# A fused four-block transformer kernel on one core: float32 scores in four row groups, gate weights broadcast by transfers, bias at the eviction, depool by gather, scalings on GpSimd, and a new order of steps

## The reference, cut to what matters

```
x = x + tanh(g0) * xattn(ctx, LN(x))          # 8 heads of 16, keys/values from ctx (256 wide), key mask
x = x + tanh(g1) * routed_attn(LN(x))         # softmax(mean(x @ Wr + br)) -> 4 of 16 heads of 64, per batch
x = x + tanh(g2) * (rmsnorm(LN(x)) @ W_in + b_in + scan(rmsnorm(ctx)[..., :128])[plug])
x = x + tanh(g3) * moe(LN(x))                 # 8 experts, 2 per token, and a shared expert

# scan: s[t] = exp(-dt) * s[t-1] + dt * bcoef * v[t];  plug[t] = clip(count of boundaries up to t, minus 1, 0, 255)
# moe, per expert e, with w the gate weight of the token for e and m its 0/1 mask:
#   h  = silu((w x) @ w1[e].T + b1[e]);   x2 = h @ w2[e].T + b2[e]
#   x3 = (w x) @ w3[e].T + b3[e];         y += x2 * x3 * m
```

## Time and profile before

| what | value |
|---|---|
| three runs | 242.54, 243.12, 247.97 us; median 243.12 |
| the profiled execution | span 242.8 us, 3827 instructions |
| TensorE matmul / weight load busy | 211.0 us (87%) / 152.9 us |
| DVE, ACT, POOL busy | 151.1, 104.6, 54.0 us |
| DMA | 17139 packets, 12.45 MB, mean 51 GB/s |

### The profile page before, as it was taken

One profiled execution on the slowest core, in us unless ns is written; L12 is line 12 of the kernel. 1 busy time (PEld: TensorE's weight loads), 2 busy tenths in 40 slices (PEclk: granted clock), 3 DMA queues, 4 the chain that ended last, 5 costly groups with the idle time before them and its releaser, 6 DMA issues.

```text
span 242.8 us, 3827 instructions
## 1 busy us (share of the span) xinstructions
PE 211.0 (87%) x1154; PEld 152.9 (63%) x1154; DVE 151.1 (62%) x464; ACT 104.6 (43%) x283; POOL 54.0 (22%) x95
## 2 busy tenths in 40 slices
PE   0786479699878679979999979999999999999995
PEld 0564366567556455757665756767786768686764
DVE  4469855547492794776558458858984764474432
ACT  2000038155204186435374546775915732483330
POOL 1360200441041000220200351114112351323332
PEclk9995555955797999996599999999999999999999
DMA  6826288011122121000011001100000000000001
GB/s 198 293 82 195 79 230 327 1 65 54 33 44 72 65 45 25 3 1 0 1 37 33 0 0 37 34 0 3 22 0 0 4 1 22 0 3 0 0 0 43
DMA packets 17139, 12.45 MB, mean 51 GB/s; under 512 B 9024, under 2 KB 16416, under 8 KB 16992
## 3 DMA queue, kind: packets, MB, share of 16 engines
q1 hardware_dynamic: 14912, 6.90, 9.9%
q10 hardware_dynamic: 2208, 5.32, 6.7%
HBM read 8.44 MB, written 0.52 MB: 37 GB/s over the span
## 4 chain that ended last, share of the span: by engine, by line
PE 52%; DVE 1%; issue 1%; ACT 0%; ACTq 0%; DVEq 0%
PE dve_bank L655 7%; PE act_bank L647 7%; PE act_bank L648 6%; PE act_bank L650 4%; PE act_bank L594 3%; PE dve_bank L584 3%; PE act_bank L576 3%; PE dve_bank L640 2%; PE dve_bank L615 2%; PE dve_bank L669 2%; PE act_bank L660 2%; PE act_bank L449 2%; PE act_bank L561 1%; PE act_bank L512 1%; PE dve_bank L660 1%; PE dve_bank L612 1%
## 5 line engine op out<-in xcount | busy, mean ns | idle before, releaser
L769 ACT ACTIVATE hx<-act_bank,we 128x256 f32<-128x256 f32 x32 | 15.2, 475 | 36.1 <-PE act_bank L650 36.1
L1065 POOL TENSOR_TENSOR ctok<-ctok,cT 128x256 f32<-128x256 f32 x28 | 20.4, 729 | 44.6 <-DVE cT L994 43.5
L913 DVE TENSOR_REDUCE mx<-dve_bank 128x2 f32<-128x512 f32 x32 | 20.7, 686 | 10.4 <-PE dve_bank L496 10.3
L725 ACT ACTIVATE pT<-act_bank 128x512 f32<-128x512 f32 x32 | 17.6, 596 | 15.1 <-PE act_bank L512 14.9
L994 DVE SCALAR_TENSOR_TENSOR cT<-dve_bank,we,hx 128x256 f32<-128x256 f32 x32 | 15.0, 482 | 10.8 <-PE dve_bank L655 10.8
L1021 POOL TENSOR_SCALAR veps<-mv 128x2 f32<-128x2 f32 x16 | 3.1, 191 | 83.9 <-DVE mv L849 83.7
L647 PE MATMUL act_bank<-xw,we 128*128 128x256 f32 x64 | 20.3, 399 | 0.0
L655 PE MATMUL dve_bank<-hx,we 128*128 128x256 f32 x64 | 19.5, 404 | 0.2 <-ACT hx L770 0.2
L987 DVE TENSOR_TENSOR xw<-xnT,dve_bank 128x512 f32<-128x512 f32 x16 | 10.9, 684 | 13.3 <-PE dve_bank L640 13.3
L648 PE MATMUL act_bank<-xw,we 128*128 128x256 f32 x64 | 19.0, 379 | 0.0
L496 PE MATMUL dve_bank<-kstack,qstack 49*128 49x256 f32 x64 | 14.9, 368 | 4.5 <-DMA qstack<-parts 4.5
(11 more groups left out here) (165 smaller groups left out, 448.2 us busy)
## 6 DMA issues: line engine op xcount, KB each, us to landing
we<-pack_e ACTq DMA_DIRECT2D x1, 1932.0 KB, 11.2
kstack<-parts SPq DMA_DIRECT2D x24, 64.0 KB, 2.6
qstack<-parts SPq DMA_DIRECT2D x24, 64.0 KB, 2.6
w2h<-head_weights SPq DMA_DIRECT2D x16, 96.0 KB, 2.4
cT<-ctx_features SPq DMA_DIRECT2D x4, 256.0 KB, 4.2
ctok<-ctx_tokens ACTq DMA_DIRECT2D x1, 1024.0 KB, 6.8
wb<-pack_b ACTq DMA_DIRECT2D x1, 594.5 KB, 6.4
xs<-x_tokens SPq DMA_DIRECT2D x4, 128.0 KB, 3.3
```

The lines of the kernel that those rows point to most:

```text
L725: act.activation(pT1[:, i].rearrange("p c t -> p (c t)"), bank[:], ACT.Exp, scale=HD1 ** -0.5).then_inc(act_done, 1)
L769: act.activation(hx[:, k % EXPERT_BUFS, 0, :], bank[:, 0:T], ACT.Silu, bias=X("b1")[:, i:i + 1])
L913: dve.tensor_reduce(mx[:, b, :, i], bank[:].rearrange("p (t s) -> p t s", t=TT), AX.X, ALU.max).then_inc(dve_done, 1)
L1065: ins = pool.tensor_tensor(yT[:, b % 2, :], yT[:, b % 2, :], prod[:, k % EXPERT_BUFS, :], ALU.add)
```

## The change

- **Scores.** s1 and st1 are float32, without the split, a head on 16 rows plus mask and maximum row (17 and 18 rows), four heads at once on four row groups of 32; a batch is two s1 steps and two st1 steps, each with four banks. Rings are 4 and 4 banks. K and Q are spread by four DMAs each and four mask rows, the maxima by one DMA, all on SP. ks and qs are set to -1 and 1 once, in place of constant rows.
- **Gate weights.** wide is gone. After gate_t, SP issues eight DMAs a batch, each spreading one row of gT (one partition) over 128 partitions of wbc, and a step xw on DVE multiplies from SBUF. gpack has 16 rows. xw has three buffers.
- **b3.** ACT adds it at the eviction, for all tokens. What that adds for tokens outside the expert is taken out again by a table, ktab = (w2 silu(b1) + b2) * b3, made once, and one matmul of 8 rows by mask minus 1 per token tile in y4.
- **Depool.** DVE scales the scan's result by the gate and adds the bias, SP stores it in DRAM, POOL gathers its rows by plug (eight indirect DMAs of 64 KB in all), and base of block three adds them. y3 keeps only the projection; plan_c is made once for all batches.
- **GpSimd.** norm's scaling, with a shift = -mean*rstd ahead of it, scale2 and base go to POOL; base is a step of its own. One-scalar operations on POOL get a second operation (times 1.0).
- **Others.** s2 goes in pairs of heads; half of the pT2 copies go to ACT; x1 to x3 have buffers for all batches; loads are issued at the start, batches 1 to 3 and ctok on ACT's queue; waits for read buffers are stated anew; ORDER is new (its line breaks are kept).

```diff
-ACT_RING, DVE_RING = 3, 5
+ACT_RING, DVE_RING = 4, 4
...
 ORDER = """
+stat:0.0 norm:0.0 gates:0.0 kv:0.0 q:0.0 base:0.0 kv:1.0 stat:1.0 s1:0.0 s1:0.1 norm:1.0 q:1.0 max1:0.0
+plan_a:0.0 stat:2.0 s1:1.0 u:0.0 st1:0.0 s1:1.1 st1:0.1 pv1:0.0 depool:0.0 pv1:0.1 max1:1.0 heads1:0.0 o1:0.0
+plan_b:0.0 y1:0.0 norm:2.0 st1:1.0 stat:0.1 q:2.0 norm:0.1 route:0.0 kv:2.0 ktab:0.0 st1:1.1 s1:2.0 consts:0.0
+qkv2:0.0 depool:1.0 s2:0.0 plan_c:0.0 s2:0.1 scale2:0.0 s1:2.1 scale2:0.1 gather:0.0 pv1:1.0 pv1:1.1 kv:3.0
...
+o1:2.0 base:2.0 stat:1.2 y1:2.0 stat:2.1 st1:3.0 gate:0.0 norm:2.1 norm:1.2 route:2.0 y3:1.0 st1:3.1
+gate_t:0.0 stat:1.3 pv1:3.0 gather:3.0 pv1:3.1 qkv2:2.0 base:2.1 norm:1.3 s2:2.0 s2:2.1 xw:0.0 scale2:2.0
+gate:1.0 scale2:2.1 heads1:3.0 up:0.0 pt2:2.0 pt2:2.1 up:0.1 pt2:2.2 pt2:2.3 xw:0.1 down:0.0 pv2:2.0 pv2:2.1
+o1:3.0 gate_t:1.0 down:0.1 y2:2.0 up:0.2 xw:0.2 base:2.2 base:3.0 stat:2.2 y1:3.0 stat:3.1 xw:0.3 shared:0.0
...
+gate:3.0 xw:2.2 up:2.2 y4:1.0 down:2.0 down:2.1 xw:2.3 gate_t:3.0 up:2.3 up:2.4 down:2.2 up:2.5 down:2.3
+down:2.4 up:2.6 up:2.7 down:2.5 xw:3.0 shared:3.0 xw:3.1 down:2.6 down:2.7 up:3.0 xw:3.2 up:3.1 up:3.2 xw:3.3
+down:3.0 up:3.3 down:3.1 up:3.4 down:3.2 up:3.5 down:3.3 up:3.6 down:3.4 up:3.7 down:3.5 down:3.6 down:3.7
+y4:2.0 y4:3.0
...
 # SyncE
-            def restack(step, dst, sources):
-                sp.wait_ge(parts_done, PARTS_AT[step] + 1)
-                for r, s in enumerate(sources):
-                    for j in range(2):
-                        lo = 64 * j + HD1 * r
-                        sp.dma_start(dst[lo:lo + HD1, b % 2].bitcast(F32),
-                                     parts[64 * j:64 * j + 64, b % 2, s, :].bitcast(F32)).then_inc(stack_in[b], 16)
+            def spread(dst, dense, landed):
+                for j in range(QUADS):
+                    sp.dma_start(dst[32 * j:32 * j + HD1], dense[32 * j:32 * j + 2 * HD1]).then_inc(landed, 16)
...
+                elif what == "gate_t":
+                    sp.wait_ge(act_done, ACT_AT[step] + 1)
+                    if b >= 2:
+                        sp.wait_ge(xw_done, (b - 1) * E // 2)
+                    for e in range(E):
+                        sp.dma_start(wbc[:, b % 2, e, :], gT[E + e:E + e + 1, b:b + 1, :].to_broadcast([1, P, T])
+                                     ).then_inc(wbc_in[b], 16)
...
 # TensorE
                 elif what == "s1":
+                    pe.wait_ge(q_stacked[b], QUADS * 16)
+                    pe.wait_ge(k_stacked[b], 2 * QUADS * 16)
+                    banks = [take_dve(nd + j) for j in range(QUADS)]
+                    for t in range(TT):
+                        for j in range(QUADS):
+                            lo, hi = 32 * j, 32 * j + ROW_MAX
+                            mm = pe.matmul(banks[j][:, t * T:(t + 1) * T], qs[lo:hi, b % 2, i, t * P:(t + 1) * P],
+                                           ks[lo:hi, b % 2, i, :], start=True, stop=True, tile_position=(lo, 0))
...
                     for t in range(TT):
-                        pe.matmul(bank[:, t * D:(t + 1) * D], xnT[2][:, b % 2, t * P:(t + 1) * P], w_in_g[:],
-                                  start=True, stop=False)
-                        for c in range(TT):
-                            mm = pe.matmul(bank[:, t * D:(t + 1) * D], pick[:, b % 2, c, t * P:(t + 1) * P],
-                                           dp[:, b, c, :], start=False, stop=(c == TT - 1))
+                        mm = pe.matmul(bank[:, t * D:(t + 1) * D], xnT[2][:, b % 2, t * P:(t + 1) * P], w_in_g[:],
+                                       start=True, stop=True)
...
                     pe.matmul(bank[:, 0:T], X("w1")[:, i * D:(i + 1) * D], xe, start=True, stop=True)
-                    pe.matmul(bank[:, T:2 * T], X("w3")[:, i * D:(i + 1) * D], xe, start=True, stop=False
-                              ).then_inc(up_read, 1)
-                    pe.matmul(bank[:, T:2 * T], b3s[:, i, :], gT[:, b, :], start=False, stop=True
+                    pe.matmul(bank[:, T:2 * T], X("w3")[:, i * D:(i + 1) * D], xe, start=True, stop=True
                               ).then_inc(act_full, 1)
...
+                        pe.matmul(bank[:, t * D:(t + 1) * D], gT[0:E, b, t * P:(t + 1) * P], ktab[:],
+                                  start=False, stop=False)
...
 # ScalarE
-                    act.copy(hx[:, k % EXPERT_BUFS, 1, :], bank[:, T:2 * T]).then_inc(act_done, 1)
+                    act.activation(hx[:, k % EXPERT_BUFS, 1, :], bank[:, T:2 * T], ACT.Identity,
+                                   bias=X("b3")[:, i:i + 1]).then_inc(act_done, 1)
...
 # VectorE
+                elif what == "xw":
...
                     dve.wait_ge(act_done, ACT_AT[("norm", b, 3)] + 1)
+                    dve.wait_ge(wbc_in[b], E * 16)
+                    dve.tensor_tensor(xw[:, pair % XW_BUFS], xnT[3][:, b % 2, :].unsqueeze(1).to_broadcast([P, 2, T]),
+                                      wbc[:, b % 2, 2 * i:2 * i + 2, :], ALU.mult).then_inc(xw_done, 1)
...
 # GpSimd
+                    for t in range(TT):
+                        ins = pool.tensor_scalar(shift[:, b, i, t:t + 1], mv[:, b, i, t, 0:1], rstd[:, b, i, t:t + 1],
+                                                 -1.0, ALU.mult, ALU.mult)
+                elif what == "norm":
+                    for t in range(TT):
+                        ins = pool.tensor_scalar(xn[:, k % XN_BUFS, t, :], x_of(i, b)[:, t, :],
+                                                 rstd[:, b, i, t:t + 1], shift[:, b, i, t:t + 1], ALU.mult, ALU.add)
+                elif what == "gather":
+                    pool.wait_ge(dp_out[b], 16)
+                    for t in range(TT):
+                        m = b * TT + t
+                        pool.indirect_dma_start(out=dpg[:, m, :], out_offset=None, in_=dp_rows[b],
+                                                in_offset=bass.IndirectOffsetOnAxis(ap=plug[:, m:m + 1], axis=0)
+                                                ).then_inc(dp_in[b], 16)
+                elif what == "scale2":
+                    pool.wait_ge(rec2_done, 2 * b + i + 1)
+                    for a in (2 * i, 2 * i + 1):
+                        for t in range(TT):
+                            ins = pool.tensor_scalar(p2[:, a, t, :], p2[:, a, t, :], rec2[:, b, a, t:t + 1], 1.0,
+                                                     ALU.mult, ALU.mult)
```

More of the change, by code:

```diff
@@ L121 @@
 NORMS = list(NORM_AT)
[L122 removed]
 XN_BUFS = 4
 EXPERT_BUFS = 3
+XW_BUFS = 3
 def expert(k):
@@ L688, in _ @@
                 bank = abank(n)
-                if USES[what][0] and what not in ("qkv2",):
+                if uses(step)[0] == 1:
                     act.wait_ge(act_full, n + 1)
@@ L837, in _ @@
                 bank = dbank(n)
-                if USES[what][1] and what not in ("kv", "q", "plan_a"):
+                if uses(step)[1] and what not in ("kv", "q", "plan_a", "s1", "ktab"):
                     dve.wait_ge(dve_full, n + 1)
@@ L923, in _ @@
                         dve.wait_ge(tanh_done, 1)
-                    residual(int(what[1]) - 1, b, bank, n + 1)
+                    residual(int(what[1]) - 1, b, bank)
                 elif what == "route":
```

659 lines of the change are left out of this document (334 added, 325 removed), and 4 rows, old and new, of the table ROW_MAX.

## The result

The changed kernel takes 392.1 us (median of four runs, 391.9 to 392.9) against 243.7 for the kernel before: a ratio of 1.609 (95% interval 1.600 to 1.618). The forecast was 220, the range 203 to 260. Single runs of the kernel before scatter from 239.5 to 251.5 us in the later comparisons, since some runs of every version come out a few per cent longer, so versions are compared by the ratio of their undisturbed runs to those of the kernel before on the same chip; about a per cent is what such a ratio tells.

The account below looks back on a forecast made before the run. TensorE was taken as the limit from 124 to 240 us, and batch 0's chain before that. From 242.8 us, 26.0 came off, 4 on for fuller engines and 0.0 for the first stage: 220.8, forecast 220, range 203 to 260.

Parts of the forecast that it names:

- the floor: Gate weight broadcast: eight SP issues plus one landing, 7.4 us a batch, hidden behind 6 to 8 us of TensorE work.
- Rival (a): Broadcast runs at its one source partition's pace, 39 us a batch, stalling DVE's xw: 345 us; chance 0.20.
- stage A: First 124 us, following batch 0's chain up to the gate: gains and losses sum to 0.0, give or take 8.
- What hides the rest in stage B: Expert stage: ACT and DVE run fuller, so a bank is late more often; 4 us added (0 to 15).
- stage B: 124 to 240 us, experts and second attention of batches 2 and 3: TensorE is the limit, 26.0 us off 116.
- I count 0 (between -15 and +3 us): First-attention scores and transposed scores: 128 float32 matmuls on four row groups, 17 us against 16 to 33 now.
- rival (c): Score matmuls' row groups do not overlap in float32 at 32 rows: +38 us, 258 us; chance 0.05.
- Norm and scalings, +7.6: Moved from DVE to POOL: normalisation +2.6 us on the chain, softmax scalings +5 for batches 0 and 1.
- The router, -4: Batch 0's router, 10.2 us after the first residual, comes 4 us earlier in the new order.
- The b3 part: Expert stage: 32 b3 matmuls removed, 16.3 us off; y4 matmuls add 3.4, fuller ACT and DVE 4.
- Term 4: Second scores always issued in pairs of heads: 2.1 us a batch instead of 3.2, 2.1 us off for two batches.
- Rival (b): POOL becomes the bound, with 58 us more work in one in-order queue: 18 us more, 239 us; chance 0.20.

Follow-up runs that it names:

- e2: Changed kernel with the gate weight rows stored to DRAM and read back by one 1 MB transfer to 128 partitions, instead of eight broadcasts: 272.2 us.
- e12: Kernel before with only the new float32 scores in sets of four banks, their new spreading and rings of 4 and 4: 262.6 us.
- e13: e12 with the transfer of the maximum row put back from SP's queue to ACT's: 251.6 us, ratio 1.023.
- e6: e2 with the arithmetic of norm and scale2 moved from POOL back to DVE: 275.9 us.
- e7: Kernel before with only the b3 change: b3 added at ACT's eviction, plus the table and its y4 matmul: 243.4 us, ratio 1.013.
- e17: Kernel before with the b3 change, its table made in the expert stage, and second scores always in pairs of heads: 248.2 us, ratio 1.012.
- e5: Changed kernel with selector matmuls in place of the broadcast, and the step order of the kernel before: 286.8 us.
- e8: e2 with the first score set of batch 2 moved behind the second scores of batch 0: 274.1 us, ratio 1.141.
- e16: e2 with the large loads moved from the start to behind the first maxima on ACT's queue: 275.7 us, ratio 1.134.
- e10: e2 with 92 matmuls that nobody reads put into TensorE's idle stretches: 269.9 us, ratio 1.112.
- e9: e5 with the arithmetic of norm and scale2 moved from POOL back to DVE: 273.5 us.

## Why the prediction was wrong

**The broadcast, "I take the floor, since four packets are too few to show a queue": this step failed.** It chose 7.4 us a batch over 39. The four packets of the earlier trace rows were the only transfer with the same source, one partition, and their pace held: a row took 4.8 us where 128 x 38 ns gives 4.9, a batch 38.9 where 39 was worked out. The stored output of the earlier trace rows, which the floor rested on, reads 128 partitions. e2, which changes nothing but this path, is 120 us shorter than the changed kernel, of the 170 between 221 and 391. Rival (a) had the place, the price of the broadcast (124 us, and TensorE waited 114) and the point from which it decides; given 0.20, it deserved most of the chance. Its 345 us missed by 46, which is the second failure below. The page of the Trainium skill that was cited against the change ("SBUF — State Buffer", section "Door 1: The DMA port swizzle") had one row at an estimated 4.8 us, and that is what a row took.

**What is left, 50 us: "so stage A stays at 124, give or take 8" failed, and so did the 4 us that were to cover "What hides the rest in stage B".** With the broadcast repaired (e2) the span is 270.9, 50 above 221. The weights of gate 0 part it; the lines are the kernel before and e2:

```profile
128.20 0.36 DVE L973 SCALAR_TENSOR_TENSOR wsel<-gexp,grec,gpack 128x8 f32<-128x8 f32 x2
```

```profile
145.62 0.41 DVE L975 SCALAR_TENSOR_TENSOR gpack<-gexp,grec,m 128x8 f32<-128x8 f32 x2
```

Ahead of that point e2 takes 17 us more, where 0 was counted; behind it 125.3 us instead of 114.6, 11 more, where 22 less were counted (some 2 us of TensorE's work moved behind it with the new order). So two thirds of the 50 us are missing in stage B. Its window, to be laid beside the second of the earlier trace rows:

```profile
154.00:262.00 108.00, 91.46 (x464) 72.01 (x456) 50.07 (x151) 57.80 (x150) 47.53 (x83) 0.89 0.14 49
```

Over the whole kernel TensorE is busy 198 us where 211 - 26 = 185 were counted, and idle 73 where the sum left 36. The rows that make up the idle time in e2 are: xn from POOL 18.3 us (7.9 before, from DVE), head weights 10.9 (1.4), the Q spread 10.5 (4.5), the K rows of batch 2 behind the head weights on SP's queue 9.3 (none): 35 us more. The busy time is 7 us less ahead of gate 0 than before. By its terms:
- Scores, "I count 0 (between -15 and +3 us)": +17 in e12, of which its trace shows 13, all ahead of gate 0. The matmuls did as told (1.15 and 2.09 us a set for 1.07 and twice that), so rival (c) is out. Some 8 to 11 of the 17 came from the maximum row on SP's queue (e13), an edit that the prediction had listed as two issues fewer (-1.2) and had not followed past the transfers ahead of it. The rest is open: the length of DVE's maxima (+1.5 was counted) gives between nothing and 4, and the rings of 4 and 4 were not tried alone.
- Norm and scalings, +7.6: POOL was faster than taken, 0.444 for 0.64 and 0.476 for 0.73, and not far from DVE's 0.405 and 0.351; only the shift was slower, 0.276 for 0.19. The wait for xn grew all the same, but it stays with DVE in POOL's place (e6), so it is no price of POOL in the new order; in the old one POOL costs some 12 to 14 us.
- The router, -4: in the changed kernel the router of batch 0 does come 5.8 us behind the first residual instead of 10.2, a gain of 4.4. It was lost again: qkv2 of batch 0 starts at 84.1 us there and at 80.5 in e2 (73.8 before), behind scores of batch 2 whose K rows stand behind qkv2's own weights on SP's queue. The prediction had asked what stands on SP's queue for the broadcast alone.
- Stage B, "I add 4 us (0 to 15)" to 26.0 off: behind gate 0 TensorE is idle 21.5 us in e2, where it was 5.1; waits for head weights (7.9) and for xn from POOL (7.6), which the sum did not have there, are most of it. It is busy 103.8 us, where 109.5 less 26 gives 84, at a mean clock of 0.88 for 1.00; at 1.00 the same work would be some 12 us less, an estimate from these two numbers. The prediction took 1.00 for the stage as it had been, and named a lower clock only as a sign of being wrong.

The b3 part alone came near: 16.3 - 3.4 - 4 = 8.9 us were counted and e7 shows 7.8 there. Term 4, pairs of scores (2.1 us a batch was the price), has the wrong sign with a ring of three: e17 is 2% slower. The table's own matmuls were not counted; in e7, which has them in the first stage, 5 us came on there.

Rival (b), POOL as the bound, did not come: POOL is 100 of 271 us busy in e2.

What stays open: how the 50 us share between order and pieces. The old order (e5) doesn't give them back, the fixes of single waits (e6, e8, e16) don't either, and what the clock is worth by itself e10 leaves within the scatter. With the old order and DVE's arithmetic (e9) the stretch behind gate 0 takes 116 us and the one ahead of it 159, so even the place of the loss depends on the order. The version with all of the waits mended at once was not tried.

## What to carry to other kernels

Price a transfer by the row whose source and destination spread over partitions as its own do, however short that row is; a transfer from one partition to 128 went at the pace of that one (39 us for 1 MB), and a detour through DRAM took 6 us. In a kernel whose engines walk one list, follow each moved transfer past all that is issued ahead of it on its new queue: one row of 8 KB cost some 8 to 11 us. Split what is left at a point that both kernels have before saying which stage failed: here the stage that looked right held two thirds of it. And where TensorE idles, look at its granted clock too: in e8 a wait of 9 us was removed and came back as slower work.

## What the runs showed of the hardware that was not expected

- Neighbouring source partitions share some 27 GB/s, on one queue or two (38.9 and 36.8 us a batch); source partitions four apart on two queues took 24.0 us, 44 GB/s in all.
- A multiplication by one scalar a partition on POOL took 642 ns for 128x128 in the kernel before (line 1037) and 413 ns with a second operation, times 1.0, beside it (line 1058); the gated bias went from 614 to 369 ns. This wasn't tried by itself; the buffers differ too.
- About as many matmul records (211 and 203) took 24.7 us at a mean granted clock of 0.67 and 33.2 us at 0.55, in the same 40 us of e2 and of e8, which differ by the place of one step.
